# Moving the first pair of row-maximum matmuls ahead of the weighted sum in each attention step

## The reference

```python
x = x + xattn(_layernorm(x), ctx)           # x (8, 1024, 512), ctx (8, 2048, 512)
...
q = (xn @ Wq.T).reshape(B, Tx, 16, 32); k = (cn @ Wk.T)...; v = (cn @ Wv.T)...
scores = jnp.einsum('bqhs,bkhs->bhqk', q, k) / np.sqrt(HEAD_DIM)
attn = jax.nn.softmax(scores, axis=-1)
out = jnp.einsum('bhqk,bkhs->bqhs', attn, v).reshape(B, Tx, C)
return out @ Wo.T + bo
...
x = x + ffn(_layernorm(x), weight, bias)    # both operands rounded to 6-bit floats in blocks of 32
```

## Time and profile before

| what | us |
|---|---|
| median of 3 runs | 4400.99 (4400.27 to 9889.38) |
| span of the profiled execution | 4390.0 |
| PE busy in it | 4263.7 (97%) |
| DVE busy | 3402.3 (78%) |
| ACT busy | 2850.7 (65%) |
| POOL busy | 2936.2 (67%) |

### The profile page before, as it was taken

How to read it: one execution, slowest core, us unless ns; L and a number is a source line. 1 busy time by engine, 2 the same in 40 slices (tenths; PEclk the granted TensorE clock), 3 DMA queues, 4 the chain that set the end, 5 groups by cost and what they waited for, 6 DMA issues and landing times.

```text
span 4390.0 us, 89201 instructions
## 1 busy us (share of the span) xinstructions
PE 4263.7 (97%) x36496; PEld 1482.1 (34%) x36496; DVE 3402.3 (78%) x3967; ACT 2850.7 (65%) x5184; POOL 2936.2 (67%) x1830
## 2 busy tenths in 40 slices
PE   4999999999999999999999999999999999999999
PEld 2322343223432234322342223422234222342223
DVE  5789667886688865889658896689866898668985
ACT  3388844887448864588655886458854688546884
POOL 2199652996539964499534995359953699426993
PEclk9999999999999999999999999999999999999999
DMA  5266742657326573356733566335664366543664
GB/s 182 70 122 128 155 149 61 126 118 191 120 61 128 118 206 103 69 118 125 192 103 77 117 126 185 107 80 120 128 175 109 80 123 130 165 113 77 126 127 110
DMA packets 193708, 539.67 MB, mean 123 GB/s; under 512 B 28737, under 2 KB 102785, under 8 KB 152082
## 3 DMA queue, kind: packets, MB, share of 16 engines
q0 software_dynamic: 43776, 318.79, 36.3%
q1 hardware_dynamic: 149522, 215.17, 15.8%
HBM read 118.32 MB, written 21.01 MB: 32 GB/s over the span
## 4 chain that ended last, share of the span: by engine, by line
PE 70%; POOL 11%; DVE 7%; DMA 5%; issue 3%; ACT 2%; SPq 0%; POOLq 0%; DVEq 0%; ACTq 0%
PE banks L1116 18%; PE banks L1128 16%; PE banks L1024 16%; PE banks L1084 12%; DVE max_parts L664 5%; PE banks L1159 3%; POOL wkT_wvT_wqT L453 3%; DMA sums<-wkT_wvT_wqT 3%; PE banks L1018 3%; PE banks L993 2%; DMA wdT<-wkT_wvT_wqT 2%; POOL values L545 1%; ACT region L894 1%; POOL region L558 1%; POOL region L531 1%
## 5 line engine op out<-in xcount | busy, mean ns | idle before, releaser
L664 DVE TENSOR_REDUCE max_parts<-banks 128x2 f32<-128x1024 f32 x2048 | 2404.5, 1220 | 362.3 <-PE banks L1084 337.4
L894 ACT ACTIVATE region<-banks 128x512 f32<-128x512 f32 x4096 | 2190.0, 609 | 424.9 <-PE banks L1116 364.4
L453 POOL TENSOR_TENSOR wkT_wvT_wqT<-region 128x1024 f32<-128x1024 f32 x528 | 1348.7, 2752 | 447.0 <-PE banks L1128 327.5
L1116 PE MATMUL banks<-queries_stacked,keys_stacked 98*32 98x512 f16 x16384 | 1267.3, 382 | 12.7 <-ACT values L878 6.2
L1128 PE MATMUL banks<-region,values 128*32 128x512 f32 x8192 | 1075.6, 598 | 18.5 <-ACT region L894 14.8
L1116 PEld LDWEIGHTS banks<-queries_stacked,keys_stacked 98*32 98x32 f16 x16384 | 399.8, 95 | 1001.7 <-ACT region L894 625.5
L1084 PE MATMUL banks<-keys_stacked,queries_stacked 33*128 33x512 f16 x4096 | 716.9, 385 | 6.9 <-DVE max_parts L664 3.5
L1024 PE MATMUL banks<-region,wkT_wvT_wqT 128*128 128x512 f16 x2304 | 558.1, 381 | 12.8 <-DMA wkT_wvT_wqT<-weights_split 10.4
L1084 PEld LDWEIGHTS banks<-keys_stacked,queries_stacked 33*128 33x128 f16 x4096 | 183.4, 93 | 616.5 <-issue 376.5
L453 POOL TENSOR_TENSOR sums<-region 128x1024 f32<-128x1024 f32 x144 | 385.7, 2821 | 0.1
L433 POOL TENSOR_TENSOR region<-row_sums_inverse,region 128x512 f16<-128x512 f32 x80 | 93.3, 1166 | 430.4 <-ACT region L857 429.9
(11 more groups left out here) (99 smaller groups left out, 3247.8 us busy)
## 6 DMA issues: line engine op xcount, KB each, us to landing
wdT<-wkT_wvT_wqT POOLq DMA_DIRECT2D x96, 1024.0 KB, 12.2
wkT_wvT_wqT<-wkT_wvT_wqT POOLq DMA_DIRECT2D x80, 1024.0 KB, 7.6
sums<-wkT_wvT_wqT POOLq DMA_DIRECT2D x72, 1024.0 KB, 7.6
wkT_wvT_wqT<-sums POOLq DMA_DIRECT2D x40, 1024.0 KB, 7.5
region<-in_x SPq DMA_DIRECT2D x24, 1024.0 KB, 8.3
wkT_wvT_wqT<-weights_split SPq DMA_DIRECT2D x8, 3072.0 KB, 20.3
keys_stacked<-region SPq DMA_DIRECT2D x384, 64.0 KB, 2.0
keys_stacked<-sums SPq DMA_DIRECT2D x384, 64.0 KB, 2.0
```

The source lines that it names most:

```text
L453: e.tensor_tensor(SUMS[dst][:, half], PR[i][:, half], PR[i + 1][:, half], ALU.add).then_inc(s_pr, 1)
L664: e.tensor_reduce(mpart[:, buf, :, a, t, c], MXB[parity], AX.X, ALU.max).then_inc(s_mxd, 1)
L894: e.activation(PR[u % 4][:, j * HALF:j * HALF + HALF], score_bank(m % NU, kt, j)[0], ACT.Exp, scale=SCALE).then_inc(s_ex, 1)
L1116: mm = e.matmul(dst[HD * t:HD * t + HD, :], KA[0:STR, ds(ka + (j * C + (u + 1) * P + HD * t), HD)], QA[0:STR, ds(qa[j], HALF)], start=True ...
```

## The change

`max_part(0)` moves in front of `outputs()` in every step that has pairs; `max_part(1)` stays at the end of the step. Neither the matmuls nor their waits change.

```diff
                     if ahead:
                         score(2)
                         score(3)
+                    if row and not ahead:
+                        max_part(0)
                     if weigh:
                         mm = outputs()
...
                     if not weigh:
                         return
                     if row:
-                        max_part(0)
+                        if ahead:
+                            max_part(0)
                         max_part(1)
```

## The result

| what | before | after |
|---|---|---|
| median of the runs beside each other, us | 4400.96 | 4507.24 |
| undisturbed runs, us | 4400.27 to 4400.99 | 4504.23 to 4508.28 |
| ratio, 95% interval | | 1.0243 [1.0226, 1.0260] |
| span of the profiled execution, us | 4390.0 | 4506.5 |

The change makes the kernel 2.4% slower, 106 us. One run of each kernel was disturbed (9889.38 before, 4901.52 after, at a granted clock of 0.851); the ratio leaves them out, and without them each median moves by about 1 us or less.

A forecast was written before the change was run, and what follows sets the result against it. It took plain steps as bound by PE and DVE waiting for each other, 2.51 us. Units 1 to 5 +11.15, unit 0 +2.72, unit 6 +0.95: 14.82 an element, 119 for eight; span 4509, plus 11 gives 4520 us, range 4440 to 4550.

The forecast's parts named there:

- ring through ACT: Third score, its exponential, waiting second score, moved pair, weighted sum, next third score: 2.68 us a plain step, before 2.24.
- the ring with DVE: Pairs and DVE's reductions wait for each other: 2.51 us a plain step before, 1.85 after; worth at most 0.10.
- PE's longer queue: PE's own work in a plain step after the change, without waits: 2.58 us.
- second rival: Third exponential comes 0.10 earlier, so PE's 2.58 us rules plain steps: 50 us in all, 4451 us; chance 0.17.
- Two more changes of shape: On PE, array shape changes four times a step instead of two, each costing about 0.1 us.
- the upper end that was chosen for the unseen step: Pair to weighted sum to next score: 0.31 + 0.88 us, by the row sum, instead of 0.23 + 0.86.
- In every plain step: Sign: in each step without row sums the second score's load waits and ACT ends the wait; weighted sums 2.68 us apart.
- Steps with row sums: Three such steps of a unit go from 10.29 to 10.48 us, set by PE's queue of 3.46 a step.
- Unit 6: Up to its step 8 it goes from 23.47 to 24.42 us, +0.95; the rest has no moved pair.
- The 11 us added to the span: Amount by which the median of the runs lies above the profiled span, added to 4509 to give 4520 us.
- loads are pulled ahead: Rival: shape change is free at the pair's new place, plain steps 2.48 us, stopped by POOL: 4370 us; chance 0.10.
- The dearer switch: Rival: shape change behind a waiting score costs 0.07 us more on 84 plain steps an element: 4567 us; chance 0.09.

The follow-up runs named there:

- the kernel with the tiny matmul: Kernel before plus one two-column matmul of zeros in the pair's shape ahead of the weighted sum, in steps with pairs: 4473.11 us, 1.0166.
- the two kernels with the tiny matmul: Kernel before plus one, or two, two-column matmuls of zeros in the pair's shape in each step with pairs: 4473.11 us and 4645.03 us.

## Why the prediction was right

The forecast was 119 us more, from a ring through ACT that takes the place of the ring with DVE; it is 106, and both mechanisms that the prediction named, the ring and the price of a change of shape, are shown. Their sizes are not those of the forecast. It had 50 us for PE's longer queue alone (the 4451 of its second rival) and 69 for the ring on top; the kernel with the tiny matmul puts about 71 on the changes of shape and leaves about 35 for the ring. The two errors have opposite signs, so that the sum came out so near is in part luck. Point by point:

- *The ring with DVE opens.* Right: neither pair waits for DVE in plain steps, and halving DVE's work changes no step of the changed kernel. Its worth was set too high: at most 0.10 us a step was 0.01 to 0.02 on average (half reductions in the kernel before). The prediction did not price the ring through the fourth exponential, 2.46 or 2.52 a step, that stood right behind it.
- *Two more changes of shape.* Right in the mechanism and in the upper end that was chosen for the unseen step. The weighted sum starts 0.32 behind the pair (1407.10 to 1407.42), its load with it and not ahead, and in the two kernels with the tiny matmul a change costs 0.10. PE's queue was put at 2.58; it is 2.63, since from the scores to the pair it is 0.55 and from a pair to whatever follows 0.32, a hundredth more in each of four pieces.
- *The ring through ACT.* Right, 2.69 for the 2.68 worked out: in step 1 the score 1408.31, the exponential 0.50 later, 0.60 long, the waiting load at 1409.46, the pair at 1409.79, the weighted sum at 1410.11, the next score 0.88 on. Two kernels that move only the pairs bear it out: with both pairs inside the ring 2.84 and 2.90, with none 2.60.
- *In every plain step.* Here the prediction failed in its size, and half of the steps do not show its own sign: the second score waits only in about every second step. In the others the exponential starts 0.44 behind its score (1405.68 to 1406.12) instead of 0.50, the bank is free in time, and PE's 2.63 rules. With it the thirteen plain steps came to 0.24 a unit less than forecast, 1.2 in units 1 to 5, and unit 0 to about 0.4 less.
- *Steps with row sums.* 10.61 (3.61, 3.50, 3.50) for 10.48: the same hundredths of PE's queue. Over units 1 to 5 they give back 0.65 of those 1.6, so that units 0 to 5 missed by 0.9 of 13.9 an element.
- *Unit 6.* To step 8 1.02 for 0.95. Behind it 0.5 came back, which the prediction set to nothing while it said that POOL gets slack: the slack was worth something just there, where ACT waits for POOL. Unit 6's last step is 3.59 in the median in place of 4.12.
- *The 11 us added to the span.* Wrong as a cause: outside the span lie 1.8 us (4508.28 and 4506.5). The execution profiled before was a short one; runs of that kernel beside the experiments went from 4390 to 4409 us, and some of that is falls of the clock at 1.4 us each. As an allowance from one execution to the median it was about right.
- *The chances.* Its cases above 4489 add up to 0.73 (0.64 and 0.09), where its last line has 0.69.

Of the rivals, the one in which loads are pulled ahead fell: the pair's load at 1408.85 starts with its matmul (1408.86), and in the traces of both kernels all loads but one do so at a change between a pair and a 32-column matmul, either way. By the rule of the Trainium skill in the page "TensorE: Matmul & The Clock Gate", section "Step-by-step: what each phase is for", it could have run ahead. In these traces loads run ahead among the 32-column matmuls, and not at these changes. The one in which the ring does not close holds for half of the plain steps. That the time lies much nearer to 4520 than to its 4451 all the same comes from PE's queue, at 2.63 and not 2.58. The dearer switch did not show.

What stays open: why the exponential starts 0.44 or 0.50 behind its score, and what decides whether the clock falls in unit 0.

## What to carry to other kernels

Before a matmul is moved to free a wait, count how often the array's shape changes along the new order, for a change costs more than the small matmul that causes it; and look for the score or tile that waits for a bank, since whatever is put between it and the work that makes the next one joins that ring. When several rings stand within a few hundredths of a microsecond of each other, opening one is worth only the distance to the next one, and closing a new one costs what it is longer than the longest of the others: here 2.69 against PE's 2.63, in half of the steps.

## What was not expected of the hardware

- A matmul of two columns with zeros, in another array shape, costs 0.2 us a step: 0.10 in each direction, the same at both places where it was tried, while one in the neighbours' shape costs nothing.
- The same pattern of instructions runs in two lengths, mostly in turn, 2.63 and 2.69, as an exponential starts 0.44 or 0.50 behind the score that it waits for.
- At the thin start of unit 0 the granted clock falls to the lower level in none to six of eight elements, in another number each execution, at some 1.4 us each. By that estimate six falls are 8 us, a part of the 10 to 20 us by which runs of one kernel differ.
